# Selective scan with an output contraction on TensorE: two time steps per matmul, and the result stored in one piece per chunk

## The chip, the cores and the metric

One Trainium2 chip, one core. The metric is the device time of one execution in microseconds. The kernel of before took 1121.71 us (median of 3 runs, 1119.78 to 1122.33).

## What is computed

Two layers on x of shape (4, 1024, 256). The first is a selective scan over 1024 time steps, for 4 batches, 256 channels d and 32 states n; the second is a token mixer over the batch axis. Cut to what matters:

```python
x = layernorm(L0_attn_x)
delta = softplus(einsum('blr,dr->bld', dt_r, W_dt) + b_dt)      # dt_r, Bm, Cm = x @ W_bc.T, split
# scan over the time t, with h of shape (batch, d, n)
dA  = exp(delta_t[:, :, None] * A[None])
dBu = (delta_t * u_t)[:, :, None] * B_t[:, None, :]
h   = dA * h + dBu
y_t = einsum('bdn,bn->bd', h, C_t)                              # the contraction over n
x1  = L0_attn_x + y + u * D_param
out = x1 + mixer(layernorm(x1))                                 # 8 tiles of 128 time steps here
```

## The kernel before, in words

**Stages.** Stage P (8 tiles of 128 time steps) normalises x, makes delta, delta*u, B and C, and stores split terms of them and `base` = x + u*D in DRAM. Stage M is the scan, in 32 chunks of `TC` = 32 time steps. Stage F is the second layer, in 8 tiles of 128 time steps that are loaded from DRAM: `y` (what stage M stored) and `base`.

**Stage M.** The 128 partitions are (batch, n): 4 times 32. A chunk has two halves of `TS` = 16 time steps (index s), and each half four steps, one for each group g of 64 channels; so a chunk has 8 steps, and the stage 256. Step G does, on each engine:

- TensorE, in this order: (1) the b-projection of L1167, 8 matmuls of 128 columns that put dBu into one of two pairs of PSUM banks; it waits until scan G-2 is done (`scan_done` >= G-1). (2) `decay_args` of L1123, 8 matmuls of the next chunk. (3) `contract` of L1136 for the half before: with g as its argument, 4 matmuls, one for each j = 0..3, each for the one time step t = 16s + 4g + j. At g = 0 it first waits until scan G-1 is done, since that finishes the half it reads; at g = 3 it increments `contract_done`.
- VectorE: adds `carry` to the first time step of each channel in PSUM (L1436), then runs the scan over 64 channels x 16 time steps (L1439, `tensor_tensor_scan`), which writes `state`. The add waits for `decay_reset` and `b_ready`, and at g = 0 for `contract_done` as well, because the state buffer is used again.
- ScalarE: exponentials of the next chunk (L1260), and once a chunk, at step 4, the copy of the contraction's result from PSUM to `y_rows` (L1288; L1301 for the last chunk).
- GpSimd: `carry` (L1018) and the reset of the first decay (L1021); once a chunk it spreads C into `c_sta` (L995), the stationary operand of the contraction.
- SyncE issues all DMAs. In a chunk: `load_md` (12, L829), `store_y` (4, L887) and `load_mu` (6, L836 and L840), each behind its own wait.

**The contraction's layout.** `c_sta` holds for each time step t a 128 x 32 stationary block, which is zero but for 4 columns, one for each batch, in slot 4*(t // 4). The four matmuls with j = 0..3 use four different 32-column strips of the array and write PSUM partitions 32j to 32j+31. So rows 4q + b of strip j hold y of batch b at t = 4q + j, and the 8 sets of a chunk add into one bank. The moving operand is `state` for one time step: 256 channels, each 16 floats (64 bytes) from the next:

```python
c_sta[k][:, t * 32:(t + 1) * 32],
sub(arena, 0, P, (2 * CHUNK_ELEMS + s * D * TS) + 4 * qq + j, (TS, D)),
```

An f32 matmul shows as two MATMUL records in the trace, so a set of 4 is 8 records.

**Stage F.** `f_load` (L280) loads a tile of `y` and one of `base` with one DMA each. GpSimd adds them (`x1`, L346), VectorE takes statistics of the sum (L590), and so on. The tiles 0 and 1 are loaded during the last chunk of stage M, tile 2 after the last `store_y`, tile 3 when all of y is stored (`m_done`), and tile lt+3 once x1 of tile lt+1 has freed its buffer, behind the store of the output of tile lt (L298) in SyncE's order.

## Time and profile before

| what | value |
|---|---|
| median of 3 runs | 1121.71 us (1119.78 to 1122.33) |
| the profiled execution | 1123.69 us |
| its span, first to last instruction | 1122.0 us |
| TensorE busy | 911.9 us (81%) |
| VectorE busy | 964.6 us (86%) |
| ScalarE busy | 460.1 us (41%) |
| GpSimd busy | 392.1 us (35%) |
| mean granted TensorE clock | 0.869 |

The page of the profile divides the span into 40 slices: stage P takes about the first 8, stage M the slices from there to the 30th, stage F the rest. A group of instructions is named by its line, engine and operation; its mean duration includes the drain of a matmul, so that the sum of durations says nothing of the rate, while start to start does.

### The profile page before, as it was taken

Reading aid. Unit: us, or ns where it says so; the run is one execution under the profiler, and the core shown is the slowest. Engines: PE = TensorE matmul, PEld = TensorE weight load, DVE = VectorE, ACT = ScalarE, POOL = GpSimd, SP = SyncE. Lnnn points to the kernel's source line nnn. Section 1 sums busy time; section 2 is a strip of 40 time slices with the busy share of each in tenths; the row PEclk is TensorE's granted clock in tenths of the full one; section 3 lists DMA queues with packets and bytes.
Section 4 is the critical chain, followed back from the end, with each engine's and each line's share of the span. In section 5 each row is a group of like instructions: output and inputs, shape, how many; then the busy total and the mean of one; then the engine's idle time right before and its main releaser. Section 6 shows DMA issues by size and latency. Waiting matters only on the chain. (4 is left out here: it accounts for less than half of the span.)

```text
span 1122.0 us, 22454 instructions
## 1 busy us (share of the span) xinstructions
PE 911.9 (81%) x7152; PEld 562.7 (50%) x7152; DVE 964.6 (86%) x1164; ACT 460.1 (41%) x887; POOL 392.1 (35%) x690
## 2 busy tenths in 40 slices
PE   5654673489999999999999999999997856666662
PEld 4343442356656656556566566565553444343442
DVE  6664664099999999999999999999998599999993
ACT  2545544434444444444444444444431333333320
POOL 6435432233333333333333333333343244444321
PEclk9675555589999999999999999999998977787786
DMA  9399995931211112121111211111142001111001
GB/s 319 64 147 205 162 135 131 134 108 50 64 52 59 54 52 64 51 62 53 59 55 50 66 51 61 55 55 57 52 139 70 16 0 57 56 56 56 19 19 37
DMA packets 206068, 85.68 MB, mean 76 GB/s; under 512 B 139220, under 2 KB 196052, under 8 KB 205268
## 3 DMA queue, kind: packets, MB, share of 16 engines
q1 hardware_dynamic: 206036, 85.30, 31.9%
q8 instruction: 15, 0.25, 0.1%
q14 instruction: 17, 0.14, 0.0%
HBM read 45.85 MB, written 39.42 MB: 76 GB/s over the span
## 5 line engine op out<-in xcount | busy, mean ns | idle before, releaser
L1439 DVE TENSOR_TENSOR_SCAN arena<-arena,psum 128x1024 f32<-128x1024 f32 x256 | 585.4, 2287 | 8.9
L1260 ACT ACTIVATE arena<-psum 128x512 f32<-128x512 f32 x512 | 281.9, 605 | 347.5 <-PE psum L1123 346.1
L1167 PEld LDWEIGHTS psum<-du_mov,b_sta 96*128 96x128 bf16 x2048 | 199.7, 130 | 237.2 <-issue 217.3
L1136 PE MATMUL psum<-arena,c_sta 128*32 128x256 f32 x2048 | 284.0, 636 | 2.7 <-DVE arena L1439 2.7
L1167 PE MATMUL psum<-du_mov,b_sta 96*128 96x128 bf16 x2048 | 271.2, 313 | 15.2 <-DVE arena L1439 15.2
L1018 POOL TENSOR_TENSOR carry<-arena 128x64 f32<-128x64 f32 x252 | 117.0, 464 | 399.2 <-DVE arena L1439 390.5
L1123 PE MATMUL psum<-delta_mov,a_sta 96*128 96x128 bf16 x2048 | 171.6, 228 | 8.3 <-ACT arena L1260 8.3
L1123 PEld LDWEIGHTS psum<-delta_mov,a_sta 96*128 96x128 bf16 x2048 | 151.9, 110 | 11.3 <-ACT arena L1260 10.2
L1021 POOL TENSOR_TENSOR arena<-zeros 128x64 f32<-128x64 f32 x256 | 78.1, 305 | 20.1
L1436 DVE TENSOR_TENSOR psum<-psum,carry 128x64 f32<-128x64 f32 x256 | 55.3, 216 | 31.3 <-DMA delta_terms<-arena 30.8
L433 PE MATMUL psum<-delta_mov,arena 128*128 128x512 f32 x128 | 75.7, 677 | 0.0
L1079 PE MATMUL psum<-arena 128*64 128x512 f32 x32 | 29.4, 1074 | 50.0 <-ACT arena L1208 50.0
L431 PE MATMUL psum<-delta_mov,arena 128*128 128x272 f32 x128 | 47.7, 459 | 23.6 <-ACT arena L503 20.4
L1136 PEld LDWEIGHTS psum<-arena,c_sta 128*32 128x32 f32 x2048 | 41.2, 109 | 31.7 <-DVE arena L1439 3.6
L418 PE MATMUL psum<-ident,arena 128*128 128x128 f32 x64 | 13.8, 387 | 50.7 <-DVE arena L606 50.7
L431 PEld LDWEIGHTS psum<-delta_mov,arena 128*128 128x128 f32 x128 | 27.1, 223 | 52.5 <-issue 46.2
L974 POOL TENSOR_TENSOR arena<-c_sta,arena 128x1024 f32<-128x1024 f32 x8 | 18.6, 2322 | 76.9 <-ACT arena L1247 76.9
L371 POOL TENSOR_TENSOR arena<-arena,delta_mov 128x1024 f32<-128x1024 f32 x16 | 30.1, 1901 | 30.7 <-ACT arena L512 30.7
L418 PEld LDWEIGHTS psum<-ident,arena 128*128 128x128 f32 x64 | 11.2, 202 | 57.0 <-issue 34.6
L1386 DVE SCALAR_TENSOR_TENSOR arena<-psum,arena 128x1024 f32<-128x1024 f32 x8 | 9.8, 1224 | 33.2 <-ACT arena L1234 33.2
L1079 PEld LDWEIGHTS psum<-arena 128*64 128x64 f32 x32 | 6.0, 218 | 63.0 <-ACT arena L1208 53.0
L1317 DVE BATCH_NORM_STATS2 arena<-arena 128x6 f32<-128x256 f32 x32 | 11.2, 411 | 29.9 <-DMA arena<-in_L_attn_x 29.9
(142 smaller groups left out, 962.8 us busy)
## 6 DMA issues: line engine op xcount, KB each, us to landing
du_terms<-arena SPq DMA_DIRECT2D x48, 256.0 KB, 3.8
du_mov<-du_terms SPq DMA_DIRECT2D x128, 96.0 KB
b_terms<-delta_mov SPq DMA_DIRECT2D x6, 1024.0 KB, 11.3
delta_terms<-arena SPq DMA_DIRECT2D x48, 128.0 KB, 5.3
delta_mov<-delta_terms SPq DMA_DIRECT2D x128, 48.0 KB
b_sta<-b_terms SPq DMA_DIRECT2D x64, 96.0 KB
arena<-in_L_attn_x SPq DMA_DIRECT2D x8, 512.0 KB, 5.5
base<-arena SPq DMA_DIRECT2D x8, 512.0 KB, 4.7
```

The costliest lines, as they stand in the source:

```text
L371: pool.tensor_tensor(dst.rearrange("p (l h i) -> p l h i", l=B, i=HK // 2), fqk[k].rearrange("p (l h i) -> p l h i", l=B, i=HK // 2), dims ...
L431: nc.tensor.matmul(bank(ba)[:, 0:COL_K], xc, w_all[:, h * WCOLS:h * WCOLS + COL_K], start=(h == 0), stop=(h == 1))
L433: mm = nc.tensor.matmul(bank(ba + 1), xc, w_all[:, h * WCOLS + COL_K:(h + 1) * WCOLS], start=(h == 0), stop=(h == 1))
L1018: ins = pool.tensor_tensor(carry[:, g, :], seg[:, :, 0], before[:, :, TS - 1], ALU.mult)
L1021: pool.tensor_tensor(seg[:, :, 0], zeros[:, :], zeros[:, :], ALU.add)\
L1079: mm = nc.tensor.matmul(bank(2)[0:R, :], w_bcT[:, h * P:h * P + R], xT[:, h * BANK:(h + 1) * BANK], start=(h == 0), stop=(h == 1))
L1123: mm = nc.tensor.matmul(psum[:, (4 + u % 2) * BANK + i * P:(4 + u % 2) * BANK + (i + 1) * P], a_sta[0:ROWS, dg * P:(dg + 1) * P], sub(delt ...
L1136: mm = nc.tensor.matmul(psum[32 * j:32 * j + 32, (6 + k) * BANK:(6 + k) * BANK + D], c_sta[k][:, t * 32:(t + 1) * 32], sub(arena, 0, P, (2 ...
L1167: mm = nc.tensor.matmul(sub(psum, 0, P, o, (4, 4), (TS, GD // 2)), b_sta[k][0:ROWS, (s * 4 + tg) * P:(s * 4 + tg + 1) * P], sub(du_mov[k], ...
L1260: nc.scalar.activation(sub(arena, 0, P, k * CHUNK_ELEMS + u * 16 * TS, (TS, 16), (D * TS, SUBS), (1, TS)), sub(psum, 0, P, (4 + u % 2) * B ...
L1436: nc.vector.tensor_tensor(firsts, firsts, carry[:, g, :], ALU.add)\
L1439: nc.vector.tensor_tensor_scan(state[s][:, seg], decay[k][:, (s * D + g * GD) * TS:(s * D + (g + 1) * GD) * TS], psum[:, 2 * (step % 2) * ...
```

## The change

The contraction takes two neighbouring time steps in one matmul: `TP` = 2, and `SETS` = 2 sets of 4 matmuls for each half. The moving operand is now 256 channels x 2 neighbouring floats (512 columns), and the stationary block holds the C of both time steps in its slots (8 columns of 32 are not zero). Each output row is then made for both time steps, of which one is wanted. The sets are issued at g = 0 and g = 2 only. `y_rows` is twice as wide; ScalarE's copy turns (channel, step) into (step, channel). GpSimd writes `c_sta` with two instructions. `store_y` writes the whole 128 x 512 tile with one DMA, unwanted values included, and `f_load` picks the wanted rows with 8 DMAs of 16 partitions x 4 batches x 1 KB, beside the one for `base`. The diff, cut to its core:

```diff
+TP = 2
+SETS = TS // (4 * TP)
+YROW = TP * D
+YLOADS = 4 * TP + 1
-        y_d = scratch("y", [B, L, D], F32)
+        y_d = scratch("y", [4, CHUNKS * 32, TP, D], F32)
-        y_rows = [sb(f"y_rows{k}", [P, D]) for k in range(2)]
+        y_rows = [sb(f"y_rows{k}", [P, 2 * D]) for k in range(2)]
         def f_load(eng, lt, k):
-            for tile, source in ((fraw[k], y_d), (fbase[k], base_d)):
-                eng.dma_start(tile.rearrange("p (b d) -> p b d", b=B),
-                              dram(source, lt * (P * D), (D, P), (L * D, B), (1, D))).then_inc(f_loaded[k], 16)
+            for j in range(4):
+                for u in range(TP):
+                    eng.dma_start(sub(fraw[k], TP * j + u, 16, 0, (D, B), (1, D), pstep=4 * TP),
+                                  dram(y_d, (j * CHUNKS * 32 + lt * P + u * B) * YROW + u * D,
+                                       (TP * B * YROW, 16), (YROW, B), (1, D))).then_inc(f_loaded[k], 16)
+            eng.dma_start(fbase[k].rearrange("p (b d) -> p b d", b=B),
+                          dram(base_d, lt * (P * D), (D, P), (L * D, B), (1, D))).then_inc(f_loaded[k], 16)
...
             def store_y(c, k):
                 settle(sp_)
                 sp_.wait_ge(S["y_evac"], c + 1)
-                for j in range(4):
-                    sp_.dma_start(dram(y_d, c * (TC * D) + j * D, (4 * D, TC // 4), (L * D, B), (1, D)),
-                                  y_rows[k][32 * j:32 * j + 32, :]).then_inc(y_stored[k], 16)
+                sp_.dma_start(dram(y_d, c * (32 * YROW), (CHUNKS * 32 * YROW, 4), (YROW, 32), (1, YROW)),
+                              y_rows[k][:, :]).then_inc(y_stored[k], 16)
...
-                    pool.tensor_tensor(
-                        sub(c_sta[k], 0, P, 0, (4 * 32 + 4, TC // 4), (32, 4), (1, B)),
...
+                    for u in range(TP):
+                        pool.tensor_tensor(
+                            sub(c_sta[k], 0, P, u * B, (4 * 32 + TP * B, 4), (32, 4), (1, B)),
...
+            def contract(k, s, sets):
+
+                for r in sets:
                     for j in range(4):
-                        t = s * TS + 4 * qq + j
-                        q = t // 4
+                        pi = SETS * s + r
                         mm = nc.tensor.matmul(
-                            psum[32 * j:32 * j + 32, (6 + k) * BANK:(6 + k) * BANK + D],
-                            c_sta[k][:, t * 32:(t + 1) * 32],
-                            sub(arena, 0, P, (2 * CHUNK_ELEMS + s * D * TS) + 4 * qq + j, (TS, D)),
-                            start=(q == 0), stop=(q == TC // 4 - 1), skip_group_check=True)
+                            psum[32 * j:32 * j + 32, (6 + k) * BANK:(6 + k) * BANK + TP * D],
+                            c_sta[k][:, (pi * 4 + j) * 32:(pi * 4 + j + 1) * 32],
+                            sub(arena, 0, P, (2 * CHUNK_ELEMS + s * D * TS) + TP * (4 * r + j), (TS, D), (1, TP)),
+                            start=(pi == 0), stop=(pi == SETS * SUBS - 1), skip_group_check=True)
...
-                                mm = contract(pc, pk, ps, [g])
-                                if g == 3:
+                                if g % 2 == 0:
+                                    mm = contract(pk, ps, [g // 2])
+                                if g == 2:
                                     mm.then_inc(S["contract_done"], 1)
...
+            def y_copy(k):
+
+                nc.scalar.copy(y_rows[k].rearrange("p (u d) -> p u d", u=TP),
+                               sub(psum, 0, P, (6 + k) * BANK, (1, TP), (TP, D))).then_inc(S["y_evac"], 1)
```

## Rows read from the trace of the kernel before

**Rows 1.** Busy us by stretch: stretch, length, PE, PEld, DVE, ACT, POOL, clock, DMA, GB/s.

```profile
256.00:836.00 580.00, 580.00 (x5642) 347.86 (x5639) 571.40 (x471) 266.46 (x499) 192.80 (x539) 1.00 0.19 58
...
840.00:853.00 13.00, 11.43 (x94) 5.09 (x91) 12.83 (x11) 0.37 (x1) 6.93 (x8) 1.00 0.14 44
```

**Rows 2.** VectorE in order of time (start, duration): edge of two chunks, last scan.

```profile
478.66 2.29 DVE L1439 TENSOR_TENSOR_SCAN arena<-arena,psum 128x1024 f32<-128x1024 f32 x1
...
481.23 2.29 DVE L1439 TENSOR_TENSOR_SCAN arena<-arena,psum 128x1024 f32<-128x1024 f32 x1
...
853.68 2.29 DVE L1439 TENSOR_TENSOR_SCAN arena<-arena,psum 128x1024 f32<-128x1024 f32 x1
```

**Rows 3.** VectorE in order of time: the first scan, and the first chunk's edge.

```profile
224.69 2.29 DVE L1439 TENSOR_TENSOR_SCAN arena<-arena,psum 128x1024 f32<-128x1024 f32 x1
...
241.81 2.29 DVE L1439 TENSOR_TENSOR_SCAN arena<-arena,psum 128x1024 f32<-128x1024 f32 x1
...
244.25 2.29 DVE L1439 TENSOR_TENSOR_SCAN arena<-arena,psum 128x1024 f32<-128x1024 f32 x1
```

**Rows 4.** Timeline of one step of stage M, TensorE and VectorE's add.

```profile
503.36 1.12 PE L1136 MATMUL psum<-arena,c_sta 128*32 128x256 f32 x8
...
504.42 1.05 PE L1167 MATMUL psum<-du_mov,b_sta 96*128 96x128 bf16 x8
...
505.63 0.21 DVE L1436 TENSOR_TENSOR psum<-psum,carry 128x64 f32<-128x64 f32 x1
...
505.84 0.62 PE L1136 MATMUL psum<-arena,c_sta 128*32 128x256 f32 x4
```

**Rows 5.** Weight loads of the last contraction, one pass of four strips each.

```profile
856.46 0.17 PEld L1136 LDWEIGHTS psum<-arena,c_sta 128*32 128x32 f32 x4 [0.28 <-issue]
856.92 0.18 PEld L1136 LDWEIGHTS psum<-arena,c_sta 128*32 128x32 f32 x4 [0.29 <-issue]
```

**Rows 6.** Contiguous f32 moving operand: two passes in stage F; ns min/median/max of one.

```profile
916.90 1.02 PE L433 MATMUL psum<-delta_mov,arena 128*128 128x512 f32 x2
...
L433 PE MATMUL psum<-delta_mov,arena x128: 592/592/1061, 867.2 to 1076.3; 128*128 128x512 f32 x128
```

**Rows 7.** Timeline at the end of stage M, and the first x1 of a loaded tile.

```profile
856.03 3.80 PE L1136 MATMUL psum<-arena,c_sta 128*32 128x256 f32 x32 [0.22 <-DVE arena L1439]
...
860.48 1.09 PE L418 MATMUL psum<-ident,arena 128*128 128x128 f32 x8 [0.65 <-DVE arena L606]
...
884.42 2.64 POOL L346 TENSOR_TENSOR arena<-du_mov 128x1024 f32<-128x1024 f32 x1 [1.22 <-ACT arena L526]
```

**Rows 8.** By line: y copy, c_sta write, y stores; ns min/median/max, first and last start.

```profile
L1288 ACT COPY y_rows<-psum x31: 368/381/389, 254.9 to 843.7; 128x256 f32<-128x256 f32 x31
...
L995 POOL TENSOR_TENSOR c_sta<-c_all,own_batch x32: 397/399/404, 200.7 to 827.4; 128x128 f32<-128x128 f32 x32
...
L887 SPq DMA_DIRECT2D y<-y_rows x128: 656/677/787, 255.4 to 862.4; - x128
```

**Rows 9.** Timeline of stage F, tile 4: its loads, x1, and VectorE around it.

```profile
938.11 0.45 SPq L280 DMA_DIRECT2D du_mov<-y  x1
938.62 1.04 SPq L280 DMA_DIRECT2D du_mov<-base  x1
...
945.31 2.50 POOL L346 TENSOR_TENSOR arena<-du_mov 128x1024 f32<-128x1024 f32 x1 [2.49 <-DMA du_mov<-base]
...
945.52 2.38 DVE L676 TENSOR_TENSOR delta_mov<-delta_mov 128x64 f32<-128x64 f32 x1
...
949.33 1.67 DVE L686 TENSOR_REDUCE delta_mov<-arena 128x16 f32<-128x128 f32 x4
...
956.49 1.40 DVE L590 BATCH_NORM_STATS2 delta_mov<-arena 128x6 f32<-128x256 f32 x4
```

**Rows 10.** Timeline of stage F: a VectorE reduction beside a GpSimd instruction.

```profile
958.42 1.21 DVE L712 TENSOR_REDUCE delta_mov<-arena 128x64 f32<-128x1024 f32 x1
...
958.59 1.02 POOL L350 TENSOR_TENSOR delta_mov<-delta_mov 128x4 f32<-128x4 f32 x1 [10.78 <-DVE delta_mov L598]
```

More of the change, by code:

```diff
@@ L262, in m_done @@
             for k in range(2):
-                eng.wait_ge(y_stored[k], 16 * 4 * (CHUNKS // 2))
+                eng.wait_ge(y_stored[k], 16 * (CHUNKS // 2))
         def dims(t, off, *d):
@@ L340, in x1 @@
             def x1(lt, k, seen):
-                pool.wait_ge(f_loaded[k], 32 * (before(lt, k) + 1))
+                pool.wait_ge(f_loaded[k], 16 * YLOADS * (before(lt, k) + 1))
                 if seen >= 2:
@@ L994, in m_pair @@
                         pool.wait_ge(S["contract_done"], 2 * c - 2)
-                    pool.tensor_tensor(
-                        sub(c_sta[k], 0, P, 0, (4 * 32 + 4, TC // 4), (32, 4), (1, B)),
-                        c_all[:, bass.ds(c * TC, TC)].rearrange("p (q j) -> p q j", j=4)
-                        .unsqueeze(3).to_broadcast([P, TC // 4, 4, B]),
-                        sub(own_batch, 0, P, 0, (0, TC // 4), (0, 4), (1, B)), ALU.mult)\
-                        .then_inc(S["cpad_ready"], 1)
+                    for u in range(TP):
+                        pool.tensor_tensor(
+                            sub(c_sta[k], 0, P, u * B, (4 * 32 + TP * B, 4), (32, 4), (1, B)),
+                            c_all[:, bass.ds(c * TC, TC)].rearrange("p (q j u) -> p q j u", j=4, u=TP)[:, :, :, u]
+                            .unsqueeze(3).to_broadcast([P, 4, 4, B]),
+                            sub(own_batch, 0, P, 0, (0, 4), (0, 4), (1, B)), ALU.mult)\
+                            .then_inc(S["cpad_ready"], 1)
                     for s in range(SUBS):
@@ L1128, in decay_args @@
                 return mm
-            def contract(c, k, s, quads):
-                for qq in quads:
+            def contract(k, s, sets):
+                for r in sets:
                     for j in range(4):
-                        t = s * TS + 4 * qq + j
-                        q = t // 4
+                        pi = SETS * s + r
                         mm = nc.tensor.matmul(
-                            psum[32 * j:32 * j + 32, (6 + k) * BANK:(6 + k) * BANK + D],
-                            c_sta[k][:, t * 32:(t + 1) * 32],
-                            sub(arena, 0, P, (2 * CHUNK_ELEMS + s * D * TS) + 4 * qq + j, (TS, D)),
-                            start=(q == 0), stop=(q == TC // 4 - 1), skip_group_check=True)
+                            psum[32 * j:32 * j + 32, (6 + k) * BANK:(6 + k) * BANK + TP * D],
+                            c_sta[k][:, (pi * 4 + j) * 32:(pi * 4 + j + 1) * 32],
+                            sub(arena, 0, P, (2 * CHUNK_ELEMS + s * D * TS) + TP * (4 * r + j), (TS, D), (1, TP)),
+                            start=(pi == 0), stop=(pi == SETS * SUBS - 1), skip_group_check=True)
                 return mm
@@ L1178, in m_pair @@
                             if not (first and k == 0 and s == 0):
-                                ps, pk, pc = (0, k, c) if s == 1 else (1, 1 - k, c - 1)
+                                ps, pk = (0, k) if s == 1 else (1, 1 - k)
                                 if g == 0:
@@ L1191, in _ @@
             pe.wait_ge(S["scan_done"], CHUNKS * STEPS)
-            contract(CHUNKS - 1, 1, 1, range(4)).then_inc(S["contract_done"], 1)
+            contract(1, 1, range(SETS)).then_inc(S["contract_done"], 1)
             phase_f_pe(pe)
@@ L1286, in m_pair @@
                             if not (isinstance(n, int) and n <= 0):
-                                act.wait_ge(y_stored[1 - k], 64 * n)
-                            nc.scalar.copy(y_rows[1 - k][:, :],
-                                           bank(7 - k)[:, 0:D])\
-                                .then_inc(S["y_evac"], 1)
+                                act.wait_ge(y_stored[1 - k], 16 * n)
+                            y_copy(1 - k)
             m_pair(0, True, False)
@@ L1299, in _ @@
             act.wait_ge(S["contract_done"], 2 * CHUNKS)
-            act.wait_ge(y_stored[1], 64 * (CHUNKS // 2 - 1))
-            nc.scalar.copy(y_rows[1][:, :], bank(7)[:, 0:D]).then_inc(S["y_evac"], 1)
+            act.wait_ge(y_stored[1], 16 * (CHUNKS // 2 - 1))
+            y_copy(1)
             phase_f_act(act)
```

2 lines of the change are left out of this document (1 added, 1 removed).

## The prediction

> **What bounds the kernel now.** I read the busy time by stretch first. From 256 to 836 us TensorE shows 580.00 us busy of 580, VectorE 571.40 (98.5%), ScalarE and GpSimd less than half, the DMA engines 0.19, and the granted clock is 1.00, 2.4 GHz [rows 1]. So two engines are in question, and busy time can't part them: VectorE's own rhythm must be found, then the rhythm that it is held to.
>
> The timeline of VectorE gives both. From the first scan at 224.69 to the last at 853.68 there are 255 intervals in 628.99 us, 2.467 us each [rows 2, 3]. In the first chunk, where the contraction starts only in the second half, eight scans from 224.69 to 244.25 take 2.445 us each, across the edge of the chunk too (2.44) [rows 3]. Later the same edge takes 481.23 - 478.66 = 2.57 [rows 2]. VectorE alone would keep 2.445; something adds 0.022 us a step.
>
> The timeline of one step shows what. TensorE starts its contraction at 503.36, the b-projection at 504.42, and the next contraction at 505.84 [rows 4]: 1.06 for the contraction and 1.42 for b-projection and decay arguments, 2.48 in all, a little more than 2.445. The b-projection's last record ends at 505.47, and the add that needs it starts at 505.63 [rows 4], so b arrives 0.16 ahead; over a chunk that margin is eaten up, and VectorE waits at its edge. TensorE bounds stage M, by 1%.
>
> **Rate of the contraction.** Two passes of four strips start 0.46 us apart for 256 columns (856.46, 856.92) [rows 5], which is 1.8 ns a column. A contiguous f32 operand of 512 columns needs 1.02 - 0.59 = 0.43 us a pass, 0.84 ns a column [rows 6]. The array is therefore not what limits the contraction: its operand jumps 64 bytes from column to column. With two passes of 0.46, what is left of the 1.06 is 0.14 of drain and change to the next part.
>
> **The new contraction.** Per half, two sets of two passes of 512 columns. No row shows pairs of neighbours. Bound below: all 512 columns at the contiguous rate, a pass of 0.43, a set X = 2 x 0.43 + 0.14 = 1.00. Bound above: each column at 1.8 ns, a pass of 0.91, X = 1.97. I take one jump for each pair, so 256 jumps, a pass of 0.43 to 0.46 and X = 1.00 to 1.06: the loss goes with the jumps, and half of them are gone.
> The Trainium skill, Advanced Engine Details and Errata, section SBUF Cachelines, says that SBUF is read in lines of 16 bytes and that two hits in a line are needed to absorb the access time; a pair is just two hits, so by that rule X is 1.00. The trace agrees in that a single hit costs twice (0.46 for 256 columns against 0.43 for 512); the pair itself no row shows.
>
> **What it is worth.** TensorE's work for two steps falls from 2 x 2.48 to 2 x 1.42 + 1.06 = 3.90, or 1.95 a step; VectorE needs 2.445. On average it bounds stage M, if the new order, bunched in every second step, never makes b late. The critical place is g = 0: there the contraction waits for the scan before, 0.06 after its end (the last scan ends at 855.97, the contraction starts at 856.03) [rows 2, 7]. The next b-projection is ready after 0.06 + X + 1.05, and the add wants it about 2.36 after that scan's end: a scan of 2.29 every 2.445 leaves 0.155 for an add of 0.21, so the add starts some 0.08 before the recorded end of the next scan [rows 3, 4]. So X may be 1.25, less a hand-over of about 0.07. With 1.06 there is no stall; at g = 2 nothing waits, and b has 0.2 us more. Stage M then takes 255 x 2.445 = 623.5 instead of 629.0: **-5.4 us**.
>
> **The other parts of the change.**
> - After the last scan the contraction of the second half shrinks from 3.80 to some 2.0 us, but TensorE's next work at 860.48 waits for VectorE's L606, not for it [rows 7]: 0. If that cover were gone it would be worth 1.8.
> - ScalarE's copy, 0.38 once a chunk [rows 8], becomes at most twice that with a strided read, 0.8. It sits before the exponentials of step 5; ScalarE is 46% busy [rows 1], so TensorE's next arguments don't wait: 0. Without that cover 32 x 0.4 = 13.
> - GpSimd writes c_sta in two instructions, at most 2 x 0.40 [rows 8], ahead of the carry of step 0, which is made three steps before its use; GpSimd is 33% busy: 0.
> - SyncE issues one y store a chunk instead of four of 0.68 [rows 8]. `load_mu` behind it starts as before, since it waits for b_ready; a lighter queue, 0. Twice the bytes of y are 128 KB more a chunk; the DMA engines are at 0.19 [rows 1]: 0.
> - In the last chunk 18 load issues stand ahead of the store of chunk 30, not 4. They go out when b of chunk 30 is made, a step or so before the last chunk's first scan (7 x 2.445 before 853.68 [rows 2], so at about 834). At 0.5 each (938.11 to 938.62 [rows 9]) they take 9 us, until the copy of chunk 30 at 843.7 [rows 8]: 0, and nothing but SyncE waits for that store.
> - After stage M the loads of tiles 2 and 3 take 18 issues, some 9 us from 861; x1 of tile 2 ran at 884.42 [rows 7]: 0.
> - For tiles 4 to 7 x1 waits for the base load: issued at 938.62, x1 at 945.31 [rows 9]. The base issue now stands behind eight y issues (16 partitions each); at 0.4 to 0.5 each it goes out 3.2 to 4.1 us after 938.11 instead of 0.5. But it then finds an empty queue: I take 4 us to land (estimate: 6.7 less the half MB of y that stood before it), so x1 starts at 945.2 to 946.6. Statistics need it at 956.49 [rows 9]; it ends by 949.1. Cover 7 us: 0. Without the cover four tiles x up to 1.3 = 5.
>
> **Sum.** 1123.7 (the profiled execution) - 5.4 = 1118.3; the median of the runs is 2.0 lower than that execution, so 1121.7 - 5.4 = **1116.3 us**. Some noise of the clock in stage F moves it by 1.5. A difference under 0.2% (2.2 us) can't be told from none here.
>
> **Rivals.**
> 1. *Stage F gains too.* While x1 runs, a VectorE instruction with two SBUF operands stands still: L676 took 2.38 at 945.52 and ended with x1, though it has 64 columns [rows 9]. That is 2.2 us in each of four tiles. A reduction isn't held up: L712 of 1.21 us ran beside GpSimd's L350 [rows 10]. Were x1 to start 1.3 to 3 us later, it would lie beside L686 (1.67 us) [rows 9], and each tile would save 1.3 to 2: 1116.3 - 4 x 1.5 = 1110.3. For: the base load is issued 2.5 to 3.5 later. Against: it lands sooner after its issue. Chance 0.20.
> The Trainium skill, SBUF — State Buffer, section Who interferes with whom, says that VectorE and GpSimd share a port pair as an exclusive lock and that a tensor_reduce never contends on trn2. The trace agrees (2.38 against 1.21); by that rule this rival gives its 1110.3 wherever x1 falls on L686.
> 2. *The pair is read no faster, slower than before.* X = 1.97; at g = 0, b comes 0.06 + 1.97 + 1.05 - 2.36 = 0.72 late in each of 63 halves. Stage M: 255 x 2.445 + 63 x 0.72 = 669, and the time 1121.7 + 669 - 629 = 1162. It decides from X = 1.34 on, where the stall eats 5.4. For: only the mean of two rates is measured, and four strips read at once. Against: rows 5 and 6. Chance 0.09.
> 3. *The clock falls.* TensorE now idles a fifth of stage M. At half clock (1.2 instead of 2.4 GHz) a pass takes 0.86, X = 1.86, 38 us of stalls if it lasted, 1154; a few per cent of the time give 1120. Against: from 840 to 853, without decay arguments, the clock stayed full [rows 1]. Chance 0.04.
> 4. *No change.* VectorE's loss at chunk edges is its own waiting, so that only a quarter of the 5.4 is got: 1120.4. Against: the first edge took 2.44 [rows 3]. Chance 0.07.
>
> **How the numbers follow.** Forecast 0.60, with 1113.5 to 1119 of its own; rival 1 adds the lower side, 1109.5 to 1113. The range 1109.5 to 1120.5 leaves out rivals 2 and most of 3, and a tail below: under 2 in 10. Faster by over 0.2% (below 1119.5): 0.60 x 0.97 + 0.20 + a little of rival 4 = 0.79. Slower: rival 2, most of 3 = 0.11. Same: 0.10.
>
> **What would show it.** Scans of stage M 2.445 apart, also at the edges of chunks; passes of the contraction 0.43 to 0.46 apart with 512 columns; TensorE idle before b-projections, released by VectorE; the last scan about 5.4 us earlier. A contraction of more than 1.3 us, or adds that come late after g = 0, would refute it. In stage F, x1 of tiles 4 to 7 relative to L650, and whether L676 still takes 2.4 us, part the forecast from rival 1.

## The result, and the profile after

The changed kernel takes 1141.99 us (median of 4 runs, 1140.86 to 1143.9) beside 1122.02 for the kernel before (4 runs, 1119.78 to 1125.58): a ratio of 1.0177, with a 95% interval of 1.0147 to 1.0207. It is slower by 20 us; the forecast was 1116.3. The profiled execution took 1143.9 us, its span is 1142.2, and its mean granted clock is 0.837 where it was 0.869. The page of the changed kernel: busy time, the granted clock in 40 slices (tenths), and three of its groups (line, engine and operation, then busy us, mean ns of one, and the idle time just before with what ended it). The row of the clock alone follows for the kernel before.

```profile
span 1142.2 us, 20272 instructions
PE 818.7 (72%) x6128; PEld 564.0 (49%) x6128; DVE 962.9 (84%) x1164; ACT 463.4 (41%) x887; POOL 388.5 (34%) x722
...
PEclk9765555589999899989989989989998877878877
...
L1449 DVE TENSOR_TENSOR_SCAN arena<-arena,psum 128x1024 f32<-128x1024 f32 x256 | 585.5, 2287 | 8.9
...
L1174 PE MATMUL psum<-du_mov,b_sta 96*128 96x128 bf16 x2048 | 289.2, 328 | 64.3 <-DVE arena L1449 64.3
...
L1143 PE MATMUL psum<-arena,c_sta 128*32 128x512 f32 x1024 | 158.1, 688 | 66.3 <-DVE arena L1449 66.3
```

```profile
PEclk9675555589999999999999999999998977787786
```

TensorE has lost 93 us of busy time (911.9 before), as intended, and waits 64 and 66 us for the scan, where it waited 15 and 3 before. Yet VectorE, which now ought to set the pace, isn't fuller: DVE 962.9 of a span that grew by 20. The row of the clock shows something that the kernel before doesn't have: between the 13th and the 28th slice, all of them stage M, PEclk drops to 8 five times. The stretches of stage M show it more closely (columns as in rows 1).

```profile
256.00:836.00 580.00, 476.86 (x4533) 337.13 (x4531) 550.20 (x453) 259.81 (x482) 179.99 (x513) 0.94 0.20 61
...
497.60:504.40 6.80, 6.27 (x34) 4.64 (x35) 5.07 (x5) 1.85 (x4) 2.01 (x6) 0.50 0.18 48
...
504.40:548.80 44.40, 36.11 (x369) 25.63 (x366) 43.71 (x37) 20.51 (x38) 14.28 (x40) 1.00 0.22 65
...
548.80:552.20 3.40, 3.14 (x15) 1.48 (x16) 2.62 (x3) 1.09 (x2) 1.32 (x4) 0.50 0.24 69
```

From 504.4 to 548.8 the clock is full and VectorE 98% busy, as in rows 1. In the stretches on both sides the granted clock is 0.50, 1.2 GHz, and VectorE is 75 and 77% busy. From the second half of chunk 1 (its first scan starts at 252.22, the first such stretch at 251.8) to the last scan there are 17 such stretches, 82 us in all; the kernel before has none in the same part. Such a drop of the granted clock to 0.50 is called a fall below.

**One stall, and where the clock is full.** Starts of the changed kernel around the fall at 548.8, from the timeline of TensorE and VectorE:

```profile
549.06 1.93 PE L1143 MATMUL psum<-arena,c_sta 128*32 128x512 f32 x8 [0.95 <-DVE arena L1449]
549.17 2.29 DVE L1449 TENSOR_TENSOR_SCAN arena<-arena,psum 128x1024 f32<-128x1024 f32 x1
...
550.93 1.66 PE L1174 MATMUL psum<-du_mov,b_sta 96*128 96x128 bf16 x8
...
552.70 0.23 DVE L1446 TENSOR_TENSOR psum<-psum,carry 128x64 f32<-128x64 f32 x1 [1.25 <-PE psum L1174]
...
552.97 2.29 DVE L1449 TENSOR_TENSOR_SCAN arena<-arena,psum 128x1024 f32<-128x1024 f32 x1
```

Two scans are 3.80 apart instead of 2.446. The add of L1446 waited 1.25 us for the b-projection, and that started 1.87 after the set of the contraction and took 1.66. The same parts at full clock, from the timeline of TensorE:

```profile
509.76 1.12 PE L1143 MATMUL psum<-arena,c_sta 128*32 128x512 f32 x8 [0.92 <-DVE arena L1449]
...
510.81 1.05 PE L1174 MATMUL psum<-du_mov,b_sta 96*128 96x128 bf16 x8
...
517.10 1.05 PE L1174 MATMUL psum<-du_mov,b_sta 96*128 96x128 bf16 x8 [0.95 <-DVE arena L1449]
...
519.72 1.07 PE L1143 MATMUL psum<-arena,c_sta 128*32 128x512 f32 x8 [1.13 <-DVE arena L1449]
```

The set takes 1.05 from start to start (509.76 to 510.81), with 512 columns a pass. That is within the forecast 1.00 to 1.06. TensorE idles twice in every four scans: 0.95 before the b-projection of g = 0 (behind the decay arguments of g = 3), and 1.13 before the set at g = 0, which waits for the scan before. From 256 to 836 us no gap is longer than 1.18. Each of the 17 falls begins in this second gap, 0.2 to 0.6 us before the scan that starts beside the set, and so each of them slows the set and the b-projection behind it.

**The balance of stage M.** From the first scan (222.87) to the last (875.81) it is 652.94 us, against 628.99 before. Of its 255 intervals, 17 are longer than 2.446 by 1.3 to 1.8 us, 26.0 in all; all of them follow a scan at g = 0. With the small ones the excess is 29.3, and 255 x 2.446 + 29.3 is 653. What TensorE and VectorE waited for from 256 to 836 us (waiting instruction, releaser: us in total, times, longest us), by the waits:

```profile
PE psum L1143 <- DVE arena L1449: 58.4, 56, 1.2
...
DVE psum L1446 <- PE psum L1174: 21.5, 15, 1.7
```

The last line is the loss: 15 adds that waited for b, 1.4 us each on average. The first is TensorE's, 56 times at g = 0.

**Stage F** (last scan to the end) takes 266.4 us instead of 268.3, so 1.9 us came back. The sum against the profiled executions: first scan 1.8 earlier, stage M +23.9, stage F -1.9, together +20.2, and 1143.9 - 1123.7 is 20.2. The loads and x1 of tile 4, in SyncE's and the engines' timeline of the changed kernel:

```profile
960.93 5.28 SPq L285 DMA_DIRECT2D du_mov<-y  x8
966.25 0.59 SPq L288 DMA_DIRECT2D du_mov<-base  x1
...
969.98 1.67 DVE L694 TENSOR_REDUCE delta_mov<-arena 128x16 f32<-128x128 f32 x4
...
970.40 2.35 POOL L354 TENSOR_TENSOR arena<-du_mov 128x1024 f32<-128x1024 f32 x1 [4.76 <-DMA du_mov<-base]
...
971.68 1.36 DVE L700 TENSOR_TENSOR delta_mov<-delta_mov 128x256 f32<-128x256 f32 x1
```

The base load is issued 5.3 us after the first y load (0.5 before [rows 9]), and x1 starts 9.5 after it instead of 7.2. It now lies beside the reduction of L694, which keeps its 1.67, and holds up only L700, for 0.93 us (1.36 where it takes 0.42 alone); before, it held up a two-operand add for 2.2 (2.38 [rows 9] instead of 0.21). The pace of the tiles is taken from one residual add (L622 before, L630 here, once a tile) to the next. The four intervals that hold the x1 of the tiles 4 to 7 take 28.6 to 28.8 us, where they took 29.4 to 29.8.

**What was costed at nothing.** By line (ns least/median/most, first and last start), and the last contraction in the timeline:

```profile
L1275 ACT COPY y_rows<-psum x32: 586/592/595, 251.9 to 880.2; 128x512 f32<-128x512 f32 x32
...
878.15 1.98 PE L1143 MATMUL psum<-arena,c_sta 128*32 128x512 f32 x16 [1.27 <-DVE arena L1449]
```

All within the bounds given: the copy 0.59 (bound 0.8), the last contraction 1.98 (forecast 2.0); by the same view one store issue takes 0.65 and c_sta 2 x 0.29 (bound 2 x 0.40). VectorE waits for none of them.

### The profile page after: what moved, and what is told of

Read it like the earlier page. It is cut to its first block and busy times, and to the rows that moved or that the text cites. A ratio compares the mean times of both kernels' runs of the same rounds, so it can differ in the third digit from the quotient of the medians.

```text
span 1142.2 us, 20272 instructions
## 1 busy us (share of the span) xinstructions
PE 818.7 (72%) x6128; PEld 564.0 (49%) x6128; DVE 962.9 (84%) x1164; ACT 463.4 (41%) x887; POOL 388.5 (34%) x722
## 5 line engine op out<-in xcount | busy, mean ns | idle before, releaser
L1268 ACT ACTIVATE arena<-psum 128x512 f32<-128x512 f32 x512 | 278.1, 595 | 364.6 <-PE psum L1131 295.8
L1174 PE MATMUL psum<-du_mov,b_sta 96*128 96x128 bf16 x2048 | 289.2, 328 | 64.3 <-DVE arena L1449 64.3
L1174 PEld LDWEIGHTS psum<-du_mov,b_sta 96*128 96x128 bf16 x2048 | 217.9, 137 | 203.1 <-DVE arena L1449 124.8
L1026 POOL TENSOR_TENSOR carry<-arena 128x64 f32<-128x64 f32 x252 | 109.6, 435 | 422.9 <-DVE arena L1449 302.8
L1143 PE MATMUL psum<-arena,c_sta 128*32 128x512 f32 x1024 | 158.1, 688 | 66.3 <-DVE arena L1449 66.3
L1131 PE MATMUL psum<-delta_mov,a_sta 96*128 96x128 bf16 x2048 | 176.8, 231 | 8.3 <-ACT arena L1268 8.3
L1131 PEld LDWEIGHTS psum<-delta_mov,a_sta 96*128 96x128 bf16 x2048 | 156.7, 112 | 12.3 <-ACT arena L1268 10.1
L1446 DVE TENSOR_TENSOR psum<-psum,carry 128x64 f32<-128x64 f32 x256 | 54.4, 213 | 54.1 <-DMA delta_terms<-arena 29.4
L1087 PE MATMUL psum<-arena 128*64 128x512 f32 x32 | 29.4, 1072 | 50.0 <-ACT arena L1216 50.0
L439 PE MATMUL psum<-delta_mov,arena 128*128 128x272 f32 x128 | 47.5, 457 | 23.4 <-ACT arena L511 20.2
L1143 PEld LDWEIGHTS psum<-arena,c_sta 128*32 128x32 f32 x1024 | 21.7, 112 | 84.6 <-DVE arena L1449 40.8
L1327 DVE BATCH_NORM_STATS2 arena<-arena 128x6 f32<-128x256 f32 x32 | 11.2, 411 | 28.7 <-DMA arena<-in_L_attn_x 28.7
```

Source lines behind the costliest of these rows:

```text
L439: nc.tensor.matmul(bank(ba)[:, 0:COL_K], xc, w_all[:, h * WCOLS:h * WCOLS + COL_K], start=(h == 0), stop=(h == 1))
L1026: ins = pool.tensor_tensor(carry[:, g, :], seg[:, :, 0], before[:, :, TS - 1], ALU.mult)
L1087: mm = nc.tensor.matmul(bank(2)[0:R, :], w_bcT[:, h * P:h * P + R], xT[:, h * BANK:(h + 1) * BANK], start=(h == 0), stop=(h == 1))
L1131: mm = nc.tensor.matmul(psum[:, (4 + u % 2) * BANK + i * P:(4 + u % 2) * BANK + (i + 1) * P], a_sta[0:ROWS, dg * P:(dg + 1) * P], sub(delt ...
L1143: mm = nc.tensor.matmul(psum[32 * j:32 * j + 32, (6 + k) * BANK:(6 + k) * BANK + TP * D], c_sta[k][:, (pi * 4 + j) * 32:(pi * 4 + j + 1) * ...
L1174: mm = nc.tensor.matmul(sub(psum, 0, P, o, (4, 4), (TS, GD // 2)), b_sta[k][0:ROWS, (s * 4 + tg) * P:(s * 4 + tg + 1) * P], sub(du_mov[k], ...
```

## The experiments

The theory after the result: the pair read is as fast as forecast and VectorE would keep its 2.446, but TensorE's idle stretches bring its clock down, and at g = 0, the one place without room, half clock makes b late. Rivals: the wider matmul or its operand brings the clock down by itself; the new storing costs; the spare time at g = 0 is too small even at full clock. The first four kernels part these. In the kernels that change the decay arguments, these are computed twice over the same place, with the same result. Falls are counted from the second half of chunk 1 to the last scan, stalls over the whole of stage M; a stall is what an interval between two scans has over 2.446, where that is more than 0.3.

### The sets at g = 1 and g = 3

```diff
-                                if g == 0:
-                                    pe.wait_ge(S["scan_done"], G)
+                                if g == 1:
+                                    pe.wait_ge(S["scan_done"], G - 1)
...
-                                if g % 2 == 0:
+                                if g % 2 == 1:
                                     mm = contract(pk, ps, [g // 2])
-                                if g == 2:
+                                if g == 3:
                                     mm.then_inc(S["contract_done"], 1)
```

> The changed kernel with its two contraction sets of a half issued at g = 1 and g = 3 instead of g = 0 and g = 2; the work is the same. Theory A (TensorE idles a fifth of stage M, so its clock falls now and then, and a fall costs time only through the contraction at g = 0, which stands between the end of a scan and the next b-projection): the clock still falls as in the changed kernel (0.94 from 256 to 836 us), but the scans stay 2.446 us apart, and the time is 1116 to 1119 us. Theory B (the stalls come from the bunched sets, whatever step they are in): 1135 to 1145 us. Theory C (they come from the loads and stores of y): 1140 us.

Measured: 1114.45 us (1112.73 to 1116.33), ratio 0.9925 (0.9898 to 0.9953). Stage M is 623.68 us from the first scan to the last, no interval over 2.446 by more than 0.01, the edges of the chunks included. The stretch of stage M, and two b-projections in TensorE's timeline:

```profile
256.00:836.00 580.00, 473.15 (x4720) 330.50 (x4712) 571.78 (x476) 268.34 (x498) 190.25 (x575) 1.00 0.22 66
...
513.25 1.05 PE L1174 MATMUL psum<-du_mov,b_sta 96*128 96x128 bf16 x8 [0.92 <-DVE arena L1449]
...
518.14 1.05 PE L1174 MATMUL psum<-du_mov,b_sta 96*128 96x128 bf16 x8 [0.95 <-DVE arena L1449]
```

The saving is all there when the sets move by one step. That was expected; that the clock is 1.00 throughout was not. TensorE is busy 473 of 580 us, no more than in the changed kernel (477), but its idle time is now one gap of up to 0.95 in every second step, 4.89 us apart (513.25 to 518.14). So not the sum of the idle time brings the clock down here, but how it is laid out, and no wider matmul does it by itself.

### Idle time filled at g = 0 and g = 3

The changed kernel with the decay arguments computed twice at these two steps, which fills TensorE's two gaps in part:

```diff
-                                    mm = decay_args(c + 1, 1 - k, u, True)
+                                    mm = decay_args(c + 1, 1 - k, u, True, 2 if g in (0, 3) else 1)
```

> The changed kernel with the decay arguments of the steps g = 0 and g = 3 computed twice over (the same values written again), 8 matmuls and some 0.45 to 0.58 us more in each of these steps, where TensorE sat idle. Theory A: the clock falls less often or never; with a clock of 1.00 through stage M the time is 1116 to 1119 us, with half of the falls 1128. Theory B or C: no gain, 1142 us or above, because work was only added.

Measured: 1118.55 us (1115.11 to 1121.24), ratio 0.997 (0.9953 to 0.9987). Stage M 629.97 us. Its stretches:

```profile
256.00:836.00 580.00, 519.15 (x5634) 382.69 (x5632) 570.32 (x473) 267.97 (x497) 191.46 (x573) 1.00 0.22 66
...
840.00:853.00 13.00, 10.76 (x52) 6.51 (x52) 10.96 (x11) 0.44 (x1) 6.06 (x6) 0.61 0.21 66
```

Some 42 us more of TensorE's busy time (519 against 477), all of it useless work, make the kernel 23 us faster, and the clock stays full until 831.6, with no stall from 256 us to there; so the spare time at g = 0 is enough at full clock. It falls only at the end, from the last chunk's edge on, where there are no decay arguments and so nothing that fills the gaps; three stalls there are 3.6 of the 6.3 us that stage M still loses. This speaks for the idle time as the cause; in which gap, the later fills show.

### The new storing alone

The kernel before, with y stored by one transfer per chunk and loaded by four per tile; the contraction is the old one.

```diff
-                for j in range(4):
-                    sp_.dma_start(dram(y_d, c * (TC * D) + j * D, (4 * D, TC // 4), (L * D, B), (1, D)),
-                                  y_rows[k][32 * j:32 * j + 32, :]).then_inc(y_stored[k], 16)
+                sp_.dma_start(dram(y_d, c * (32 * D), (CHUNKS * 32 * D, 4), (D, 32), (1, D)),
+                              y_rows[k][:, :]).then_inc(y_stored[k], 16)
...
-            for tile, source in ((fraw[k], y_d), (fbase[k], base_d)):
-                eng.dma_start(tile.rearrange("p (b d) -> p b d", b=B),
-                              dram(source, lt * (P * D), (D, P), (L * D, B), (1, D))).then_inc(f_loaded[k], 16)
+            for j in range(4):
+                eng.dma_start(sub(fraw[k], j, 32, 0, (D, B), (1, D), pstep=4),
+                              dram(y_d, (j * CHUNKS * 32 + lt * P) * D,
+                                   (B * D, 32), (D, B), (1, D))).then_inc(f_loaded[k], 16)
```

> The kernel before with the second half of the change alone: the contraction reads one time step as before, y_rows (128 x 256) is stored by one transfer per chunk, and the last stage's loads pick the rows with 4 transfers of 32 partitions and one for base. Theory A: nothing in stage M, scans 2.467 us apart as before, clock 1.00; stage F within 3 us; 1118 to 1123 us. Theory C (the slower time comes from the stores and loads): 1135 to 1142 us.

Measured: 1122.65 us (1120.88 to 1133.18), ratio 1.0023 (0.9997 to 1.0048), stage M 625.85, stage F 270.8.

```profile
256.00:836.00 580.00, 579.66 (x5659) 348.93 (x5656) 571.80 (x473) 265.43 (x498) 197.10 (x545) 1.00 0.19 59
```

Stage M keeps its full clock and loses nothing, so the storing has no part in the 24 us. The store that is twice as wide wasn't run alone, but the kernel with the sets at g = 1 and g = 3 has it and loses nothing either. That the storing shortened stage M by 3 us and lengthened stage F by 2.5 was not expected. The 3 us lie at the edges of the chunks: there 28 intervals of the kernel before are over 2.446 by some 0.12, 3.4 us in all, and here 2 are, 0.25 us. So fewer stores alone win over half of what the forecast gave to a lighter TensorE; why isn't shown.

### The kernel before with half of its contraction

The old contraction of 256 columns, but only at g = 0 and g = 2. Half of y isn't computed, so its time is no rival to the others; it has nearly the gaps of the changed kernel (0.6 to 0.95 and 1.0) without its pairs, its 512 columns or its stores.

```diff
-                                mm = contract(pc, pk, ps, [g])
-                                if g == 3:
+                                if g % 2 == 0:
+                                    mm = contract(pc, pk, ps, [3 * g // 2])
+                                if g == 2:
                                     mm.then_inc(S["contract_done"], 1)
```

> The kernel before with the contraction sets at g = 1 and g = 3 left out (a set of single time steps of 256 columns at g = 0 and one at g = 2 are left; half of the contraction is not computed). TensorE's work per step is that of the changed kernel at full clock, 1.95 us, without pairs of time steps, without 512 columns and without the new stores. Theory A: TensorE idles as much, so the clock falls as in the changed kernel (some 17 stretches of 3.4 to 7 us in stage M); a set of 256 columns takes 1.1 us at half clock instead of 1.86, so each fall costs some 0.8 us instead of 1.6: 1125 to 1132 us. Theory D (the operand of pairs or 512 columns is what makes the stalls or the falls): clock 1.00 and 1116 us.

Measured: 1145.91 us (1144.82 to 1147.5), ratio 1.0218 (1.0189 to 1.0248). Stage M 652.07 us. The stretch, then a set and the b-projection behind it in a fall that begins at 498.4:

```profile
256.00:836.00 580.00, 482.00 (x4535) 355.57 (x4533) 550.41 (x453) 254.81 (x482) 182.18 (x506) 0.91 0.18 55
...
498.31 1.12 PE L1136 MATMUL psum<-arena,c_sta 128*32 128x256 f32 x8 [0.95 <-DVE arena L1440]
...
499.36 1.89 PE L1167 MATMUL psum<-du_mov,b_sta 96*128 96x128 bf16 x8
```

Half of the contraction is gone and the kernel is 24 us slower than with all of it. The clock falls 35 times, and 36 stalls of 0.69 to 0.87 make 28.3 us. A stall costs less than in the changed kernel, and the rows say why: this set takes 1.05 in the fall (498.31 to 499.36; 1.08 in one that begins ahead of the set, 263.03 to 264.11), as at full clock (1.05, 488.53 to 489.58), and it is the b-projection that takes 0.8 more. Passes of single time steps are 0.43 to 0.49 apart at either clock. Passes of pairs are 0.43 to 0.47 apart at full clock and 0.86 at half (490.63 and 491.49 in the kernel with both sets at g = 1, below). So the change has made the contraction depend on the clock, which it hardly did before. The falls come twice as often as I took, so that the total lies over what I gave for it. Of the rivals, that the pairs or the wide matmul bring the clock down is out.

### Which of the two gaps

The fill at one step alone:

```diff
-                                    mm = decay_args(c + 1, 1 - k, u, True)
+                                    mm = decay_args(c + 1, 1 - k, u, True, 2 if g == 0 else 1)
```

and `2 if g == 3 else 1` in the second kernel.

> The changed kernel with the decay arguments computed twice at g = 0 alone, so that the idle stretch of 1.1 us ahead of the contraction at g = 0 shrinks to some 0.6, while the one ahead of the b-projection of the same step stays 0.95. Theory P (the clock falls because the two idle stretches of a half stand close together, 2.1 us of idle within some 4 us, where the version with the sets at g = 1 and g = 3 has the same idle time spread evenly): fewer falls than 16, perhaps 0 to 5, 1117 to 1126 us. Theory Q (only the longer stretch of 1.1 us matters): no falls, 1116 us. Theory R (it is the mean work of stage M that counts): some 8 falls, 1130 us.

> The same filling at g = 3 alone: the idle stretch of 0.95 us ahead of the b-projection of g = 0 shrinks to some 0.4, the one of 1.1 ahead of the contraction stays. Theory P: as with the filling at g = 0 alone, 1117 to 1126 us. Theory Q: the falls stay, 1142 us. Theory R: 8 falls, 1130 us.

Measured with the fill at g = 0: 1119.02 us (1115.27 to 1122.67), ratio 0.9965 (0.9948 to 0.9981), stage M 628.85, two falls, both at the last chunk. With the fill at g = 3: 1141.78 us (1139.76 to 1143.47), ratio 1.0167 (1.0141 to 1.0193), stage M 653.14, 18 falls and 18 stalls of 27.9 us in all. First the kernel with the fill at g = 0, then that at g = 3, each with the stretch of stage M and the two gaps:

```profile
256.00:836.00 580.00, 491.75 (x5182) 356.72 (x5179) 571.47 (x473) 269.10 (x499) 190.89 (x575) 1.00 0.22 65
...
517.71 1.05 PE L1175 MATMUL psum<-du_mov,b_sta 96*128 96x128 bf16 x8 [0.89 <-DVE arena L1450]
...
520.15 1.07 PE L1144 MATMUL psum<-arena,c_sta 128*32 128x512 f32 x8 [0.50 <-DVE arena L1450]
```

```profile
256.00:836.00 580.00, 496.38 (x4980) 356.17 (x4976) 548.89 (x454) 258.62 (x481) 181.07 (x532) 0.95 0.20 61
...
515.13 1.05 PE L1175 MATMUL psum<-du_mov,b_sta 96*128 96x128 bf16 x8 [0.41 <-DVE arena L1450]
...
517.75 1.93 PE L1144 MATMUL psum<-arena,c_sta 128*32 128x512 f32 x8 [1.13 <-DVE arena L1450]
```

The same work added at either place, and 23 us between them. Of the expectations, that both gaps count alike fell; that the longer one, ahead of the set at g = 0, decides fits these two kernels. With 0.89 and 0.50 left the clock holds, with 0.41 and 1.13 it falls; but the sum of the two differs as well (1.39 and 1.54), so these two kernels don't say which of the two counts.

### Both sets at g = 1

```diff
-                                if g == 0:
-                                    pe.wait_ge(S["scan_done"], G)
+                                if g == 1:
+                                    pe.wait_ge(S["scan_done"], G - 1)
...
-                                if g % 2 == 0:
-                                    mm = contract(pk, ps, [g // 2])
-                                if g == 2:
+                                if g == 1:
+                                    mm = contract(pk, ps, range(SETS))
                                     mm.then_inc(S["contract_done"], 1)
```

> The version with the sets at g = 1 and g = 3, but with both sets of a half at g = 1, 3.4 us of work in that step and 1.4 in each of the three others. At full clock b is ready 4.5 us after the scan two steps before, 0.3 before it is wanted, so the scans stay 2.446 us apart. Theory P: idle now gathers at the end of one half and the start of the next (three stretches of about 1 us in a row), the clock falls at least as often as in the changed kernel, and a fall that meets the step of the bursts costs 1 to 2 us: 1125 to 1150 us. Theory R or the rival that only waiting at g = 0 harms: clock 1.00 and 1115 us.

Measured: 1142.35 us (1140.97 to 1146.68), ratio 1.0174 (1.0152 to 1.0196). Stage M 655.02 us, 12 stalls of 31.2 in all. The stretch of stage M, two gaps at full clock, then both sets at half clock and the add behind them:

```profile
256.00:836.00 580.00, 471.76 (x4546) 338.72 (x4544) 548.44 (x455) 259.74 (x482) 182.03 (x534) 0.95 0.21 61
...
517.63 1.05 PE L1174 MATMUL psum<-du_mov,b_sta 96*128 96x128 bf16 x8 [0.92 <-DVE arena L1448]
520.07 1.05 PE L1174 MATMUL psum<-du_mov,b_sta 96*128 96x128 bf16 x8 [0.95 <-DVE arena L1448]
...
490.63 3.64 PE L1143 MATMUL psum<-arena,c_sta 128*32 128x512 f32 x16
...
495.41 0.23 DVE L1445 TENSOR_TENSOR psum<-psum,carry 128x64 f32<-128x64 f32 x1 [2.62 <-PE psum L1174]
```

Outside of the half-clock stretches VectorE doesn't stall, so the burst fits in at full clock. But the clock falls 11 times, nine of them ahead of the last chunk, where no gap is longer than 0.95. So the length of one gap is not the rule either; nor did a single longer gap bring the clock down, of 1.40 in the kernel before (ahead of L1136 at 846.24) and of 1.32 in the kernel with the sets at g = 1 and g = 3 (at 831.21). What is seen: one gap of 0.95 every 4.89 us never brought the clock down before the last chunk; gaps in neighbouring steps, 0.95 and 1.13 or 0.92 and 0.95 again and again, did. Which measure of idle time the clock follows stays open.

### The y loads in eight transfers, alone

The kernel before, its y load of a tile split in eight:

```diff
-            for tile, source in ((fraw[k], y_d), (fbase[k], base_d)):
-                eng.dma_start(tile.rearrange("p (b d) -> p b d", b=B),
-                              dram(source, lt * (P * D), (D, P), (L * D, B), (1, D))).then_inc(f_loaded[k], 16)
+            for i in range(8):
+                eng.dma_start(sub(fraw[k], i, 16, 0, (D, B), (1, D), pstep=8),
+                              dram(y_d, lt * (P * D) + i * D,
+                                   (8 * D, 16), (L * D, B), (1, D))).then_inc(f_loaded[k], 16)
+            eng.dma_start(fbase[k].rearrange("p (b d) -> p b d", b=B),
+                          dram(base_d, lt * (P * D), (D, P), (L * D, B), (1, D))).then_inc(f_loaded[k], 16)
...
```

> The kernel before, with nothing changed but the loads of y in the last stage: 8 transfers of 16 partitions each instead of one, so that x1 of the tiles 4 to 7 starts some 2.5 us later in its tile and lies beside VectorE's four reductions (L686) instead of beside two-operand instructions. Theory S (that position is what made the last stage's tiles 28.7 us long instead of 29.7 in the changed kernel): tiles of 28.7 us, and 1117 to 1120 us in all. Rival (the shorter tiles come from something else in the change): tiles of 29.7 us and 1122 us.

Measured: 1120.33 us (1116.25 to 1122.3), ratio 0.9975 (0.996 to 0.999). The four intervals take 28.7, 28.5, 28.7 and 28.8 us, as in the changed kernel, stage F 266.9, and stage M stays at 629.02. Tile 4:

```profile
975.08 1.67 DVE L689 TENSOR_REDUCE delta_mov<-arena 128x16 f32<-128x128 f32 x4
...
975.53 2.35 POOL L349 TENSOR_TENSOR arena<-du_mov 128x1024 f32<-128x1024 f32 x1 [4.80 <-DMA du_mov<-base]
```

With the old contraction and the old layout of y, more issues ahead of the base load are enough for x1 to lie beside the reduction. The 2 us of stage F are a matter of when GpSimd starts, not of how y is stored.

### Where the base load stands among the eight

The kernel with the sets at g = 1 and g = 3, once more, and with the base load ahead of all y loads, or behind five of the eight:

```diff
...
+            for i in range(9):
+                if i == 5:
+                    eng.dma_start(fbase[k].rearrange("p (b d) -> p b d", b=B),
+                                  dram(base_d, lt * (P * D), (D, P), (L * D, B), (1, D))).then_inc(f_loaded[k], 16)
+                if i < 8:
+                    y_part(i // TP, i % TP)
```

and `i == 0` to have it first.

> The version with the sets at g = 1 and g = 3, once more and in more rounds, to set it against the two that follow: 1113 to 1116 us, scans 2.446 us apart, clock 1.00 through stage M, the last stage's tiles 28.7 us.

> The same, with the load of base issued ahead of the 8 loads of y instead of behind them. The last transfer is then one of 64 KB instead of 512 KB, issued at the same time, so x1 of the tiles 4 to 7 starts 1 to 2.5 us earlier. Theory S (x1's place among VectorE's instructions sets what it costs, now 1.0 us a tile on the instruction behind the four reductions): 1 us earlier, at the start of the reductions, tiles of 27.8 us and 1111 us; more than 1.2 us earlier it holds up a two-operand instruction again, tiles of 29.7 us and 1118 us. Rival (tiles depend on how many transfers there are, not on x1's place): 28.7 us and 1114.5 us.

> The same, with the load of base issued behind the first five of the 8 loads of y. x1 of the tiles 4 to 7 starts 0.5 to 1.5 us earlier than with base last, later than with base first. Theory S: near the start of the reductions, tiles of 27.8 to 28.3 us and 1111 to 1113 us. Rival: 28.7 us and 1114.5 us.

| base load | us (lowest to highest) | ratio to before, 95% | the four intervals, us |
|---|---|---|---|
| last | 1113.98 (1112.61 to 1117.64) | 0.9924 (0.9899 to 0.9949) | about 28.7 each |
| first | 1118.13 (1113.41 to 1125.97) | 0.996 (0.9939 to 0.9982) | 28.0, 29.8, 29.8, 29.8 |
| sixth | 1112.41 (1108.23 to 1114.95) | 0.9907 (0.9879 to 0.9935) | 28.9, 29.4, 28.0, 28.0 |

x1 with what VectorE does beside it: with the base load first (tile 5),

```profile
966.61 2.56 POOL L357 TENSOR_TENSOR arena<-du_mov 128x1024 f32<-128x1024 f32 x1 [3.02 <-DMA du_mov<-y]
966.88 2.58 DVE L690 TENSOR_TENSOR delta_mov<-delta_mov 128x256 f32<-128x256 f32 x1
```

and with the base load sixth (tile 6):

```profile
997.80 2.35 POOL L357 TENSOR_TENSOR arena<-du_mov 128x1024 f32<-128x1024 f32 x1 [4.20 <-DMA du_mov<-y]
997.95 1.67 DVE L697 TENSOR_REDUCE delta_mov<-arena 128x16 f32<-128x128 f32 x4
...
999.64 0.79 DVE L703 TENSOR_TENSOR delta_mov<-delta_mov 128x256 f32<-128x256 f32 x1
```

In the first, x1 holds up an add for the whole of its time, and a tile takes 29.8; in the second it falls nearly whole on the reduction, the add behind takes 0.79, and a tile takes 28.0. Between the tile with x1 best and worst placed lie 1.8 us. The version with the base load sixth, 1112.41, beats both kernels: by 0.9% (0.65 to 1.2) the one before. Against the base load last its lead, 1.6 us, is within the two intervals.

The repeat of the sets at g = 1 and g = 3 has one thing more to say. Here the clock does fall twice, in the last chunk. The second of the two stretches, and the timeline inside it:

```profile
847.20:850.60 3.40, 3.40 (x16) 1.15 (x14) 3.37 (x3) 0.00 (x0) 0.04 (x1) 0.50 0.00 0
...
846.68 2.29 DVE L1449 TENSOR_TENSOR_SCAN arena<-arena,psum 128x1024 f32<-128x1024 f32 x1
...
847.84 1.94 PE L1143 MATMUL psum<-arena,c_sta 128*32 128x512 f32 x8
...
849.13 2.29 DVE L1449 TENSOR_TENSOR_SCAN arena<-arena,psum 128x1024 f32<-128x1024 f32 x1
```

The set takes 1.94 at half clock, and the scans are 2.45 apart all the same: stage M is 623.69. With the sets at g = 1 and g = 3 none of them stands between a scan's end and the next b, and a fall costs nothing. So moving the sets does two things: it keeps the clock up, and it takes the cost from a fall.

## Why the prediction was wrong

**Wrong: that the clock stays full.** The step that failed is "With 1.06 there is no stall": it took X at full clock in every half, and rival 3, which says otherwise, was wrong in its chance and in its price. The clock fell in 17 of the 63 halves, and each fall made b 1.3 to 1.8 us late.

- Its chance, 0.04, rested on one stretch: 840 to 853 at clock 1.00 [rows 1], without decay arguments. TensorE is busy 11.43 us of the 13 there, so 12% idle, less than the 18% from 256 to 836 us after the change: it couldn't speak against a fall at more. Nor does a sum of idle time decide; the two kernels with equal busy shares (477 and 473 us of 580, clocks 0.94 and 1.00) show that.
- Its price took X = 1.86 at half clock, and X is 1.87 (549.06 to 550.93). But what lies between the scan's end and the next b is the set and the b-projection, and the latter slows too: its matmuls start 0.213 us apart instead of 0.109, some 0.8 us more over the eight. With both slower a fall costs 1.3 to 1.8 us, not the 0.61 of the prediction.
- "A few per cent of the time give 1120": the half-clock share is 82 of 653 us, an eighth, but a share of the time is not the share of the sets that are hit. The falls begin in the gap ahead of the set at g = 0, so that 17 of them stalled 17 of 63 halves, over a quarter. Their 26 us are what the falls cost.

**Right: the pair read.** X = 1.05 at full clock against 1.00 to 1.06. One jump for each pair is what it costs: the passes of the last contraction are 0.43 to 0.46 apart with 512 columns, as they were with 256 single ones. The Trainium skill, Advanced Engine Details and Errata, section SBUF Cachelines, says that two hits in a line are needed to absorb the access latency, and the trace now agrees for pairs, as far as 0.43 is also the contiguous pass [rows 6]. Rival 2 is out. The passes of [rows 5] were themselves taken at half clock (from 856.5 to 859.5 the granted clock is 0.50), which single time steps don't show and pairs do: the doubling of the set at half clock is a price of the pairs.

**Right: VectorE's floor.** Where the clock holds or doesn't matter, stage M is 623.68 and 623.69 us, against 623.5 forecast. Rival 4 is out, since the whole 5.3 us is got. That TensorE alone sets the chunk edges isn't shown, since the new storing alone took 3 us off them. The -5.4 in stage M was right for a kernel with the same sets one step later, which gave 1114.45; that this is below 1116.3 is stage F's doing.

**Right, but narrowly: the room at g = 0.** X up to 1.25 less 0.07 was forecast to fit, and at full clock no interval is over 2.446 by more than 0.2. It isn't quite nothing: behind g = 0 in the second halves of chunks the kernel filled at g = 0 and g = 3 is 0.07 us over in 28 intervals, 2.1 us in all, and the kernel with the sets at g = 1 and g = 3 isn't; why only the second halves isn't shown. And 0.1 us of room is no room for half clock.

**Stage F: a term mis-sized, and rival 1 has happened.** I took 0.4 to 0.5 for a y issue; eight of them take 5.28 us, 0.66 each. The base load was then issued 5.3 us after the first, not 3.2 to 4.1, and took about 4 to land as I had said, so x1 came 9.5 after the first issue and not 7.1 to 8.5. That moves it onto the reductions. The gain was 0.9 a tile in the four (114.8 us together for 118.4), less than the 1.3 to 2 of rival 1, because 0.9 to 1.2 us of x1 still fall on the add behind; the two tiles after them take 1.0 more together (26.0 and 22.7 against 22.8 and 24.9), and the part ahead of them 0.7 more. The Trainium skill, SBUF — State Buffer, section Who interferes with whom, says that a reduction never contends with GpSimd and a two-operand instruction does; the rows agree: the reductions of L694 keep their 1.67 beside x1, while with the base load first the add of L690 takes 2.58 in place of 0.42.

**Right at nothing:** the copy, c_sta, the store and the last contraction, as shown above, and the loads at the last chunk, for which VectorE doesn't wait.

## What to carry to other kernels

When a change takes work off TensorE, ask where its idle time will lie and what stands right behind it: here some 100 us of idle in stage M were free as one gap in every second step, and cost 24 us as two gaps in neighbouring steps with critical work behind them. Count how many critical pieces a fall would meet, and not the share of the time: a fall began where TensorE idled, and so just ahead of the piece that waited. Price a possible half clock by the whole chain from the wait to the consumer (set and b-projection), and move work with a late deadline out of that chain; the move was worth 28 us here and costs nothing. A GpSimd instruction that holds up VectorE's two-operand instructions can be timed by what precedes its load in the DMA queue: 1.8 us a tile lay between its best and its worst place.

## What was not expected of the hardware

- The granted clock fell to 0.50 with no idle gap longer than 1.18 us from 256 to 836 us, and in one kernel with none over 0.95 up to the last chunk, while single gaps of 0.95 did nothing until the last chunk.
- Useless matmuls can pay: 42 us more of TensorE work at g = 0 and 3 made the kernel 23 us faster, and the part of them at g = 0 alone did the same.
- Half as much contraction made the kernel before 24 us slower, only by the clock.
- An f32 operand read in pairs, each pair 64 bytes from the next, goes at about the contiguous rate: 512 columns a pass in what 256 single ones need (1.05 against 1.06 for a set). At half clock the single ones keep 1.05 to 1.11, and the pairs take 1.87.
